# A two-layer graph network on one core: variances by five vector operations in place of 26, and twelve tiles of edge sums moved ahead of a wait

## The chip, the cores and the metric

The kernel runs on one core of a Trainium2 chip. The metric is the device time of one execution in microseconds; the time before is the median of three runs.

## The reference

```python
edge_index = stack([src, dst])                    # 3125 nodes, 53125 edges (loops among them), sorted by dst
h = maximum(layernorm(x), 0)                      # x is 3125 x 128; eps 1e-5
# layer 0: twelve steps of a network over the edges
h = tanh(h @ W_in + b_in)
deg = clip(segment_sum(1, dst), 1)
for step in range(12):
    agg = segment_sum(h[src], dst) / deg
    diff = tanh(gelu(agg @ W1 + b1) @ W2 + b2)
    h = h + (diff - relu(clearance) * h) * 0.5
x = x + h
# layer 1: two graph convolutions with further self loops and degree norms
h = maximum(layernorm(x), 0)
h = relu(gcn_conv(h, G1, gb1)); x = x + gcn_conv(h, G2, gb2)

def layernorm(x): m = mean(x); v = var(x); return (x - m) / sqrt(v + eps)
```

## The kernel before

Nodes are cut into 25 tiles of 128 (the last has 53), and the tiles into seven groups (four tiles each, then three, then two). The sum over edges is a product with an adjacency matrix of counts, `adj`, which the kernel builds in SBUF from the edge list. Node values enter that product as two f16 parts, `hi` and `lo`, so a tile of sources costs two matmuls of 128x512 for one group of destinations.

**The entry.** The edge list is searched for the start of each of 625 windows of five destination nodes. Meanwhile VectorE takes BN_STATS of every tile of `x` (`row_statistics`, L1346): six numbers a row, which are count, mean and count times variance of the even and of the odd elements. `variances` (L1349 to L1353) turns them into mean and variance, 25 times BN_AGGR and one add of eps. ScalarE takes the root (L1150), VectorE its reciprocal and the shift (`norm_factors`, L1415 to L1419), and ScalarE (L1156) and GpSimd (L662) then normalize the rows. The helper `link` makes VectorE wait for its own last result.

**The batches.** 52 batches of 12 windows build `adj`. For each, VectorE writes one-hot columns (`one_hots`, L1447), TensorE multiplies them into three PSUM banks (`window`, L795), and ScalarE moves the banks into `adj` (`evict`, L1174). Even batches use banks 0 to 2, odd ones banks 3 to 5. Between the batches TensorE does the first layer of the network and, when `adj` is far enough, parts of the first step's edge sums: `first_sums(g, part)` (L812) adds tiles `part` of sources into the bank of group g. A 625th window is done alone at the end (L849) and moved by a short eviction (L1197). When that has ended (`s_last[2]`), DMAs are started from SP (L545, the row of inverse degrees for all partitions) and from ScalarE's queue (the copy of a short tile within `adj`, `s_pair`).

**The first step.** On TensorE follow, in program order: a load of a flag from SBUF into a register (L851, `value_load`), the branch on it (L853) over a path that this graph does not take, the wait for `s_last[2]`, a small product that numbers blocks of edges of the last group (L1025, into bank 5, `s_boff`), and tiles 12 to 23 of the third group (`first_sums(2, ...)`, 24 matmuls). Then `s_owner` is waited for, which VectorE's `block_owners` (L1561 to L1574) gives from the numbering, and the sums of the fourth group begin.

The steps 1 to 10 are a loop, step 11 and the two convolutions follow.

Of the kernel before, what the change touches and what calls it, by code (L numbers as in the profile page):

```python
# [24 lines left out]
ALU = mybir.AluOpType  # L25
# [5 lines left out]
FULL = NODES // P  # L31
LAST = NODES - FULL * P
TILES = FULL + 1
# [3 lines left out]
FEAT = 128  # L37
# [3 lines left out]
EPS = 1e-5  # L41
# [25 lines left out]
BATCHES = WINDOWS // BATCH  # L67
# [6 lines left out]
EARLY_FROM = LO_AT[0] + 2  # L74
EARLY_TILES = 2
EARLY_LATE = EARLY_TILES * (BATCHES - ENTRY_BATCHES)
EARLY_PARTS = [(0, FULL - 1), (0, FULL), (0, EARLY_LATE - FULL)]
assert 0 < EARLY_LATE - FULL < FULL
assert EARLY_FROM + FULL <= ENTRY_BATCHES
PACK = 4096  # L80
# [8 lines left out]
OPEN = 1  # L89
# [15 lines left out]
SETS = PLACES // 2  # L105
SET_NODES = 2 * PLACE_NODES
# [5 lines left out]
def gnn_kernel(nc, x, src, dst, W_in, b_in, W1, b1, W2, b2, clearance, G1, gb1, G2, gb2, out):  # L112
    ctx = ExitStack()
    with ctx:
# [62 lines left out]
        ln_a = col(TILES)  # L177
        ln_b = col(TILES)
# [7 lines left out]
        def early_col(n, like=guess_and_stats):  # L186
# [4 lines left out]
        tail_first, tail_bound, tail_found, tail_start, tail_blocks, tail_mask2 = (  # L191
            early_col(SETS)[0:SET_NODES, :] for _ in range(6))
# [27 lines left out]
        stats = scratch[:, o:o + TILES * 6].rearrange("p (k s) -> p k s", s=6)  # L220
# [6 lines left out]
        tail_order = act_out[0:SET_NODES, o:o + SET_NODES]  # L227
# [148 lines left out]
        s_ev = [sem(f"windows_stored{u}") for u in range(2)]  # L376
# [354 lines left out]
        def _(pe):  # L731
# [60 lines left out]
            def window(buf, w, bank, place):  # L792
                b, i_ = w // RUN, w % RUN
                target = bank[:, 0:BANK_WIN * WROW].rearrange("p (k c) -> p k c", k=TILES)
                return nc.tensor.matmul(target[:, :, place * WIN:(place + 1) * WIN], Lb[buf][:, b, :, i_],  # L795
                                        Rb[buf][:, b, :, i_].rearrange("p (k d) -> p k d", d=WIN),
                                        start=True, stop=True)
# [8 lines left out]
            def first_sums(g, part):  # L806
                c0, n = SPANS[g]
                for at in range(*part):
                    k = K_FIRST[at][0]
                    for values in (hi, lo):  # L810
                        if values is hi or k != SHORT:
                            mm = nc.tensor.matmul(ps[:, FIRST_BANK[g], 0:n], values[:, k, :], adj[:, k, c0:c0 + n],  # L812
                                                  start=(at == 0 and values is hi),
                                                  stop=(k == SHORT or (g == 0 and at == FULL - 2 and values is lo)))
                return mm
# [31 lines left out]
            pe.wait_ge(s_last[0], 1)  # L847
            pe.wait_ge(s_ev[0], BATCHES // 2 + OPEN)
            window(0, 0, ps[:, 0, :], 0).then_inc(s_last[1], 1)  # L849

            missed = pe.value_load(flag[0:1, 0:1], min_val=0, max_val=1)  # L851

# [152 lines left out]
            def first_step():  # L1005
                def rest_and_short(g):
                    c0, n = SPANS[g]
                    bank = ps[:, REST_BANK[g], 0:n]

                    if g == 0:  # L1010
                        k = K_FIRST[FULL - 1][0]
                        nc.tensor.matmul(bank, hi[:, k, :], adj[:, k, c0:c0 + n], start=True, stop=False)
                        nc.tensor.matmul(bank, lo[:, k, :], adj[:, k, c0:c0 + n], start=False, stop=False)
                    with pe.If(missed != 0):
                        with pe.Fori(0, TILES) as r:
                            add_rest(0, g, bank, r)
                    nc.tensor.matmul(bank, hi[:, SHORT, :], adj[:, SHORT, c0:c0 + n], start=False, stop=True
                                     ).then_inc(s_agg, 1)

                def tail_check_sum():  # L1020
                    pe.wait_ge(s_valid, 1)
                    nc.tensor.matmul(ps[:, 2, 0:1 + CAP], ones_col.broadcast_to((P, P)), tail_check,
                                     start=True, stop=True).then_inc(s_checked, 1)

                nc.tensor.matmul(ps[0:SET_NODES, 5, 0:SETS], tail_order, tail_blocks, start=True, stop=True  # L1025
                                 ).then_inc(s_boff, 1)
                first_sums(2, (EARLY_PARTS[2][1], FULL))
                pe.wait_ge(s_owner, 1)
                for j in range(SETS):
                    nc.tensor.matmul(ps[:, 5, 16 + 4 * j:20 + 4 * j], owner[j], block_rows[:, j, :], start=True, stop=True)  # L1030
                    mm = nc.tensor.transpose(ps[:, 5, 64 + j * SET_NODES:64 + (j + 1) * SET_NODES], owner[j],
                                             ident[0:SET_NODES, 0:SET_NODES])
                mm.then_inc(s_ownerT, 1)
                first_sums(3, (0, 2 * HEAD))
                pe.wait_ge(s_pair, 16)
                for g in range(3):
                    rest_and_short(g)
                first_sums(3, (2 * HEAD, FULL))
                hidden(0, 0)
                rest_and_short(3)  # L1040
                first_sums(4, (0, HEAD))
                outputs(0, 0)
                hidden(0, 1)
                tail_check_sum()
                first_sums(4, (HEAD, 2 * HEAD))
                outputs(0, 1)
                hidden(0, 2)
                first_sums(4, (2 * HEAD, FULL))
                rest_and_short(4)
                outputs(0, 2)  # L1050
                hidden(0, 3)
                first_sums(5, (0, SPLIT))
                outputs(0, 3)
                hidden(0, 4)
                first_sums(5, (SPLIT, FULL))
                rest_and_short(5)
                first_sums(TAIL, (0, FULL))
                rest_and_short(TAIL)
                outputs(0, 4)
                hidden(0, 5)  # L1060
                hidden(0, TAIL)
                edge_sums(1, 0, (s_hi, s_lo), NG, (0, HEAD))
                outputs(0, TAIL - 1)
                outputs(0, TAIL)
                pe.wait_ge(s_tflag, 1)
# [221 lines left out]
        def _(dve):  # L1287
            chain = [0]

            def link(ins):  # L1290
                chain[0] += 1
                ins.then_inc(s_v, 1)
                dve.wait_ge(s_v, chain[0])
# [53 lines left out]
                return last_  # L1347

            def variances():  # L1349
                for k in range(TILES):  # L1350
                    last_ = V.bn_aggr(mv[:, k, :], stats[:, k, :])  # L1351
                link(last_)
                return V.tensor_scalar(ln_b[:, :], mv[:, :, 1], EPS, None, ALU.add)  # L1353

            def key_group(g):
                dve.wait_ge(s_wedges[g], 16)
# [58 lines left out]
            def norm_factors():  # L1415
                dve.wait_ge(s_std, 1)
                link(V.reciprocal(ln_a[:, :], ln_a[:, :]))
                V.scalar_tensor_tensor(out=ln_b[:, :], in0=mv[:, :, 0], scalar=-1.0, in1=ln_a[:, :], op0=ALU.mult,
                                       op1=ALU.mult).then_inc(s_ln, 1)  # L1419


# [465 lines left out]
```

## Time and profile before

| | |
|---|---|
| median of 3 runs | 1267.23 us (1266.03 to 1267.9) |
| the profiled execution | 1266.38 us, its span 1264.8 us |
| TensorE busy | 1227.2 us, 97% of the span |
| VectorE busy | 411.5 us |
| ScalarE busy | 306.4 us |
| GpSimd busy | 570.8 us |
| chain that ended last | TensorE 91%, VectorE 6% |

The profile has rows of what each engine did and when, in microseconds from the start of the span. The chain is followed back from the last instruction, at each step to what released it. PEclk is the granted clock of TensorE as a share of 2.4 GHz.

### The profile page before, as it was taken

How to read it: one execution, taken by the hardware profiler on the slowest of the kernel's cores; microseconds unless marked ns; L12 is line 12 of the kernel's file. 1: busy time of each engine (PE TensorE's matmuls, PEld its weight loads, DVE VectorE, ACT ScalarE, POOL GpSimd, SP SyncE). 2: the span in 40 equal slices, each digit the busy share in tenths (PEclk: the TensorE clock that was granted, in tenths of full speed). 3: DMA queues.
4: the chain of work that ended last, by engine and by line, in shares of the span. 5: the costliest groups of instructions: out<-in, count | busy, mean ns of one | idle time of the engine just before them, and what ended most of it. 6: DMA issues, size and time to landing. Idle time of an engine off the chain costs nothing.

```text
span 1264.8 us, 17221 instructions
## 1 busy us (share of the span) xinstructions
PE 1227.2 (97%) x6757; PEld 695.0 (55%) x6757; DVE 411.5 (33%) x853; ACT 306.4 (24%) x455; POOL 570.8 (45%) x426
## 2 busy tenths in 40 slices
PE   3899999999999999999999999999999999999998
PEld 1776565564564655645556456455564564555645
DVE  7999323131130231311302214113122142382412
ACT  1898222130131221301312113113131131130100
POOL 6700104827718448277284481772845818600000
PEclk8799999999999999999999999999999999999999
DMA  4000211222222312222222222231222223420101
GB/s 103 3 1 1 66 34 37 36 56 40 35 59 35 56 38 35 58 36 34 60 35 54 40 35 59 35 47 47 36 52 42 35 58 67 92 62 1 52 17 35
DMA packets 106136, 54.58 MB, mean 43 GB/s; under 512 B 13238, under 2 KB 104473, under 8 KB 105964
## 3 DMA queue, kind: packets, MB, share of 16 engines
q0 software_dynamic: 46352, 23.46, 14.4%
q1 hardware_dynamic: 57958, 29.48, 8.7%
q10 hardware_dynamic: 1782, 1.06, 0.3%
q8 instruction: 26, 0.43, 0.1%
q14 instruction: 18, 0.15, 0.0%
HBM read 32.53 MB, written 21.04 MB: 42 GB/s over the span
## 4 chain that ended last, share of the span: by engine, by line
PE 91%; DVE 6%; issue 1%; DMA 1%; ACT 1%; POOL 0%; DVEq 0%; ACTq 0%; POOLq 0%
PE ps L907 63%; PE ps L971 11%; PE ps L961 10%; PE ps L812 4%; DVE scratch L1447 3%; PE ps L795 2%; PE ps L1082 1%; PE ps L950 1%; DMA adj<-packed_scratch,adj 1%; DVE adj L1301 0%; DVE state L1730 0%; DVE lo L1430 0%; DVE cols L1351 0%; DVE adj L1392 0%; ACT adj L1174 0%
## 5 line engine op out<-in xcount | busy, mean ns | idle before, releaser
L907 PE MATMUL ps<-adj,hi 128*128 128x512 f16 (+2 forms) x2000 | 710.7, 367 | 0.0
L907 PE MATMUL ps<-adj,lo 128*128 128x512 f16 (+2 forms) x1920 | 693.8, 367 | 0.0
L684 POOL DMA_INDIRECT scratch<-state_scratch,tail_rows x264 | 390.6, 1480 | 390.4 <-DMA state_scratch<-state 313.2
L907 PEld LDWEIGHTS ps<-adj,hi 128*128 128x128 f16 x2000 | 194.3, 97 | 218.1 <-issue 12.9
L907 PEld LDWEIGHTS ps<-adj,lo 128*128 128x128 f16 x1920 | 186.8, 97 | 213.2 <-issue 14.6
L1622 DVE TENSOR_TENSOR ps<-ps,bias 128x512 f32<-128x512 f32 (+2 forms) x84 | 53.8, 641 | 488.9 <-PE ps L971 488.9
L1219 ACT ACTIVATE scratch<-ps 128x512 f32<-128x512 f32 (+2 forms) x84 | 46.3, 552 | 574.3 <-DVE ps L1622 573.3
L1210 ACT ACTIVATE scratch<-ps,b1c,cols 128x512 f32<-128x512 f32 (+2 forms) x156 | 107.3, 740 | 176.9 <-PE ps L961 176.1
L971 PEld LDWEIGHTS ps<-w,scratch 128*128 128x128 f32 (+1 forms) x1152 | 138.4, 190 | 14.0 <-issue 5.3
L971 PE MATMUL ps<-w,scratch 128*128 128x128 f32 (+1 forms) x1152 | 143.6, 276 | 0.1
L684 POOL DMA_INDIRECT entry<-state_scratch,tail_rows x88 | 129.7, 1474 | 26.8 <-issue 26.8
L961 PE MATMUL ps<-scratch,w 128*128 128x512 f32 (+2 forms) x336 | 137.8, 538 | 0.0
L1615 DVE TENSOR_TENSOR scratch<-ps,scratch 128x512 f32<-128x512 f32 (+1 forms) x72 | 47.6, 661 | 180.9 <-PE ps L961 130.5
L1447 DVE TENSOR_TENSOR scratch<-scratch 128x1536 f16<-128x1536 f16 (+1 forms) x106 | 91.7, 938 | 0.3 <-PE ps L795 0.3
L961 PEld LDWEIGHTS ps<-scratch,w 128*128 128x128 f32 x336 | 58.9, 190 | 37.8 <-issue 28.7
L1174 ACT ACTIVATE adj<-ps 128x1500 f16<-128x1500 f32 (+1 forms) x52 | 76.0, 1478 | 9.6 <-PE ps L795 9.3
L1629 DVE SCALAR_TENSOR_TENSOR state<-state,cols,scratch 128x512 f32<-128x512 f32 (+2 forms) x84 | 58.3, 694 | 49.7 <-ACT scratch L1219 49.5
L795 PE MATMUL ps<-scratch 128*128 128x125 f16 x625 | 56.9, 253 | 9.2 <-DVE scratch L1447 8.1
L1430 DVE SCALAR_TENSOR_TENSOR lo<-state,cols,hi 128x512 f16<-128x512 f32 (+2 forms) x91 | 59.9, 672 | 9.5 <-ACT hi L1110 8.8
L795 PEld LDWEIGHTS ps<-scratch 128*128 128x128 f16 x625 | 47.6, 112 | 24.4 <-DVE scratch L1447 21.3
L1110 ACT ACTIVATE hi<-state,cols 128x512 f16<-128x512 f32 (+2 forms) x84 | 53.2, 671 | 19.5 <-PE ps L950 11.7
L812 PE MATMUL ps<-adj,hi 128*128 128x512 f16 (+2 forms) x167 | 57.1, 354 | 0.0
(218 smaller groups left out, 420.3 us busy)
## 6 DMA issues: line engine op xcount, KB each, us to landing
state_scratch<-state SPq DMA_DIRECT2D x55, 256.0 KB, 2.3
scratch<-state_scratch,tail_rows POOLq DMA_INDIRECT x264
state_scratch<-state SPq DMA_DIRECT2D x11, 192.0 KB, 2.0
scratch<-rdeg_scratch SPq DMA_DIRECT2D x1, 1562.5 KB, 8.8
entry<-state_scratch,tail_rows POOLq DMA_INDIRECT x88
state<-in_x_dram SPq DMA_DIRECT2D x5, 256.0 KB
scratch<-in_x_dram SPq DMA_DIRECT2D x5, 256.0 KB
x_scratch<-state SPq DMA_DIRECT2D x5, 256.0 KB, 3.7
```

What stands on the lines that cost most here:

```text
L684: nc.gpsimd.indirect_dma_start(tail_sum[i], None, state_dram, bass.IndirectOffsetOnAxis(ap=tail_rows[:, at:at + 1], axis=0), compute_op=AL ...
L795: return nc.tensor.matmul(target[:, :, place * WIN:(place + 1) * WIN], Lb[buf][:, b, :, i_], Rb[buf][:, b, :, i_].rearrange("p (k d) -> p ...
L812: mm = nc.tensor.matmul(ps[:, FIRST_BANK[g], 0:n], values[:, k, :], adj[:, k, c0:c0 + n], start=(at == 0 and values is hi), stop=(k == SHO ...
L907: return nc.tensor.matmul(bank, values[:, k, :], adj[:, k, c0:c0 + n], start=is_first, stop=is_last)
L961: nc.tensor.matmul(ps_hid_tail[h] if g == TAIL else ps_hid[h][:, 0:n], w1[:, h * FEAT:(h + 1) * FEAT], agg[g == TAIL][:, 0:n], start=True, ...
L971: mm = nc.tensor.matmul(ps_out[g == TAIL][0:m, i * FEAT:(i + 1) * FEAT], hid_of(g, h)[:, i * P:i * P + m], w2[:, h, :], start=(h == 0), st ...
L1174: nc.scalar.activation(adj[:, :, bass.ds((i * 2 + u) * BATCH * WIN, BATCH * WIN)].rearrange("p k (b c) -> p b k c", b=BANKS), ps[:, 3 * u: ...
L1210: nc.scalar.activation(hid_of(g, h)[:, 0:n], ps_hid_tail[h] if g == TAIL else ps_hid[h][:, 0:n], ACT.Gelu, bias=b1c[:, h:h + 1], scale=now ...
L1430: return V.scalar_tensor_tensor(out=lo[:, k0:k1, :], in0=values[:, k0:k1, :], scalar=0.0 if factor is None else factor, in1=hi[:, k0:k1, : ...
L1447: last_ = V.tensor_tensor(buf[:, 0:b, :, 0:w], c_.broadcast_to((128, b, m, w)), k_.broadcast_to((128, b, m, w)), ALU.is_equal)
L1622: V.tensor_tensor(p_, p_, bias_of(1, nt), ALU.add).then_inc(s_bias, 1)
L1629: V.scalar_tensor_tensor(out=tiles_of(state, g), in0=tiles_of(state, g), scalar=now_keep, in1=act_out[:, 0:n_], op0=ALU.mult, op1=ALU.add) ...
```

## The change

Two edits. `variances` computes mean and variance of all 25 tiles at once from the six numbers: sum and difference of the two half means, sum of the two second moments, the difference squared times 32, and their sum divided by 128. What it leaves as the mean is twice the mean, and `norm_factors` multiplies by -0.5 in place of -1. The block numbering and tiles 12 to 23 of the third group stand ahead of the load of the flag and of the wait for the last eviction; they wait for the last odd eviction (`s_ev[1]`), which frees bank 5.

```diff
-EARLY_PARTS = [(0, FULL - 1), (0, FULL), (0, EARLY_LATE - FULL)]
+EARLY_PARTS = [(0, FULL - 1), (0, FULL), (0, FULL)]
...
             window(0, 0, ps[:, 0, :], 0).then_inc(s_last[1], 1)
+            pe.wait_ge(s_ev[1], BATCHES // 2 + OPEN)
+            nc.tensor.matmul(ps[0:SET_NODES, 5, 0:SETS], tail_order, tail_blocks, start=True, stop=True
+                             ).then_inc(s_boff, 1)
+            first_sums(2, (EARLY_LATE - FULL, FULL))
 
             missed = pe.value_load(flag[0:1, 0:1], min_val=0, max_val=1)
...
-                nc.tensor.matmul(ps[0:SET_NODES, 5, 0:SETS], tail_order, tail_blocks, start=True, stop=True
-                                 ).then_inc(s_boff, 1)
-                first_sums(2, (EARLY_PARTS[2][1], FULL))
                 pe.wait_ge(s_owner, 1)
...
             def variances():
-                for k in range(TILES):
-                    last_ = V.bn_aggr(mv[:, k, :], stats[:, k, :])
-                link(last_)
-                return V.tensor_scalar(ln_b[:, :], mv[:, :, 1], EPS, None, ALU.add)
+                mean_e, mean_o, dev_e, dev_o = (stats[:, :, i] for i in (1, 4, 2, 5))
+                V.tensor_tensor(mv[:, :, 0], mean_e, mean_o, ALU.add)
+                V.tensor_tensor(ln_b[:, :], dev_e, dev_o, ALU.add)
+                link(V.tensor_tensor(ln_a[:, :], mean_e, mean_o, ALU.subtract))
+                link(V.scalar_tensor_tensor(out=ln_a[:, :], in0=ln_a[:, :], scalar=FEAT / 4, in1=ln_a[:, :], op0=ALU.mult,
+                                            op1=ALU.mult))
+                link(V.tensor_tensor(ln_b[:, :], ln_b[:, :], ln_a[:, :], ALU.add))
+                return V.tensor_scalar(ln_b[:, :], ln_b[:, :], 1 / FEAT, EPS, ALU.mult, ALU.add)
...
-                V.scalar_tensor_tensor(out=ln_b[:, :], in0=mv[:, :, 0], scalar=-1.0, in1=ln_a[:, :], op0=ALU.mult,
+                V.scalar_tensor_tensor(out=ln_b[:, :], in0=mv[:, :, 0], scalar=-0.5, in1=ln_a[:, :], op0=ALU.mult,
                                        op1=ALU.mult).then_inc(s_ln, 1)
```

On VectorE, between the end of the statistics and the second batch of one-hots (`cols` holds `mv`, `ln_a` and `ln_b`, `scratch` the statistics and the one-hots), this stood before:

```order
L1346 BN_STATS scratch<-state 128x6 x2
L1363 TENSOR_SCALAR adj<-adj 128x125 [waits slot_edges_ready]
L1364 TENSOR_SCALAR adj<-adj 128x125
L1351 BN_AGGR cols<-scratch 128x2 [waits vector_chain]
L1351 BN_AGGR cols<-scratch 128x2 x24
L1353 TENSOR_SCALAR cols<-cols 128x25 [waits vector_chain]
L1447 TENSOR_TENSOR scratch<-scratch 128x1536 [waits windows_multiplied0,window_keys_copied,one_hot_counts_made]
L1447 TENSOR_TENSOR scratch<-scratch 128x1500
L1417 RECIPROCAL cols<-cols 128x25 [waits deviations_ready]
```

and this stands there now:

```order
L1347 BN_STATS scratch<-state 128x6 x2
L1368 TENSOR_SCALAR adj<-adj 128x125 [waits slot_edges_ready]
L1369 TENSOR_SCALAR adj<-adj 128x125
L1352 TENSOR_TENSOR cols<-scratch 128x25 [waits vector_chain]
L1353 TENSOR_TENSOR cols<-scratch 128x25
L1354 TENSOR_TENSOR cols<-scratch 128x25
L1355 SCALAR_TENSOR_TENSOR cols<-cols 128x25 [waits vector_chain]
L1357 TENSOR_TENSOR cols<-cols 128x25 [waits vector_chain]
L1358 TENSOR_SCALAR cols<-cols 128x25 [waits vector_chain]
L1452 TENSOR_TENSOR scratch<-scratch 128x1536 [waits windows_multiplied0,window_keys_copied,one_hot_counts_made]
L1452 TENSOR_TENSOR scratch<-scratch 128x1500
L1422 RECIPROCAL cols<-cols 128x25 [waits deviations_ready]
```

26 instructions with one wait between them have become six with three waits between them; nothing around them has moved.

On TensorE, from the last window (bank 0) to the block owners, this stood before (the first gap is the path that is branched over, the second the other 22 matmuls of tiles 12 to 23):

```order
L795 MATMUL ps<-scratch 128x25x5 [waits windows_stored0,last_window_one_hots]
L851 TENSOR_LOAD flag
L851 ISA x2
L853 COMPARE_AND_BRANCH
...
L1025 MATMUL ps<-cols,scratch 92x2 [waits weights_loaded,last_window_stored]
L812 MATMUL ps<-adj,hi 128x512
L812 MATMUL ps<-adj,lo 128x512
...
L1030 MATMUL ps<-cols,scratch 128x4 [waits tail_block_owners_ready]
```

and this stands there now (the first gap is the other 22 matmuls, the second the path that is branched over):

```order
L795 MATMUL ps<-scratch 128x25x5 [waits windows_stored0,last_window_one_hots]
L851 MATMUL ps<-cols,scratch 92x2 [waits windows_stored1]
L812 MATMUL ps<-adj,hi 128x512
L812 MATMUL ps<-adj,lo 128x512
...
L855 TENSOR_LOAD flag
L855 ISA x2
L857 COMPARE_AND_BRANCH
...
L1031 MATMUL ps<-cols,scratch 128x4 [waits tail_block_owners_ready,weights_loaded,last_window_stored]
```

The numbering product and 24 matmuls have moved from behind the load, the branch and the wait for the last window's eviction to ahead of all three, behind a wait for the last odd batch's eviction.

## Rows read from the trace of the kernel before

**Rows 1.** The page: busy time of the engines and share of the span.

```profile
PE 1227.2 (97%) x6757; PEld 695.0 (55%) x6757; DVE 411.5 (33%) x853; ACT 306.4 (24%) x455; POOL 570.8 (45%) x426
```

**Rows 2.** Busy time by stretch: length, busy time of each engine, PEclk, DMA share, GB/s.

```profile
53.00:100.00 47.00, 42.43 (x411) 33.17 (x411) 46.95 (x57) 45.05 (x44) 5.48 (x3) 0.98 0.04 2
100.00:134.00 34.00, 32.15 (x301) 21.80 (x301) 31.51 (x39) 29.02 (x22) 0.00 (x0) 1.00 0.00 1
300.00:1200.00 900.00, 899.87 (x4654) 493.58 (x4653) 232.25 (x493) 175.69 (x295) 464.30 (x313) 1.00 0.26 46
```

**Rows 3.** The chain that ended last, 28 to 56 us: start, length, what.

```profile
29.43 1.67 DVE cols L1351 x25
...
44.34 1.21 PE ps L795 x12
...
46.39 0.86 PE ps L795 x12
```

**Rows 4.** VectorE in order of time, 27 to 44.5 us: start, length, what.

```profile
29.34 1.75 DVE L1351 BATCH_NORM_AGGREGATE cols<-scratch 128x2 f32<-128x6 f32 x25
31.12 0.18 DVE L1353 TENSOR_SCALAR cols<-cols 128x25 f32<-128x25 f32 x1
31.23 1.81 DVE L1447 TENSOR_TENSOR scratch<-scratch 128x1536 f16<-128x1536 f16 x2
...
40.24 0.18 DVE L1398 COPY adj<-ps 125x25 f32<-125x25 f32 x1
40.46 0.18 DVE L1399 TENSOR_TENSOR adj<-ps,adj 125x25 f32<-125x25 f32 x1
...
41.53 0.18 DVE L1410 TENSOR_REDUCE cols<-adj 125x1 f32<-125x25 f32 x1
41.62 0.17 DVE L1411 TENSOR_SCALAR adj<-adj 125x25 f32<-125x25 f32 x1
```

**Rows 5.** ScalarE's root in order of time, with its idle time before and the releaser.

```profile
31.34 0.22 ACT L1150 ACTIVATE cols<-cols 128x25 f32<-128x25 f32 x1 [1.37 <-DVE cols L1353]
```

**Rows 6.** TensorE by stretch: length, busy time, PEclk, DMA share, GB/s.

```profile
44.00:45.00 1.00, 0.74 (x8) 0.60 0.00 0
...
51.00:52.00 1.00, 1.00 (x13) 0.82 0.00 0
...
55.00:56.00 1.00, 1.00 (x14) 0.98 0.00 0
```

**Rows 7.** All engines in order of time around the last evictions, 128 to 140 us.

```profile
132.32 1.48 ACT L1174 ACTIVATE adj<-ps 128x1500 f32 x1 [0.23 <-PE ps L795]
...
132.87 0.23 PE L795 MATMUL ps<-scratch 128*128 128x125 f16 x1
133.69 0.31 ACT L1197 ACTIVATE adj<-ps 128x125 f16<-128x125 f32 x1
...
134.05 0.32 PE L1025 MATMUL ps<-cols,scratch 92*92 92x2 f32 x2 [0.95 <-ACT adj L1197]
...
136.44 0.22 DVE L1571 TENSOR_SCALAR cols<-cols 92x2 f32<-92x2 f32 x1
```

**Rows 8.** TensorE's sequencer: duration in ns (min/median/max), first and last start.

```profile
L851 PEldq TENSOR_LOAD <-flag x1: 496/496/496, 132.3 to 132.3; - x1
...
L853 PEldq COMPARE_BRANCH  x1: 367/367/367, 133.1 to 133.1; - x1
...
L1014 PEldq COMPARE_BRANCH  x7: 200/207/323, 143.4 to 188.5; - x7
```

**Rows 9.** What the first step needs next: times of use, and a DMA's landing.

```profile
142.88 0.15 DVE L1642 TENSOR_SCALAR cols<-cols 128x1 f32<-128x1 f32 x1 [6.22 <-DMA scratch<-rdeg_scratch]
...
147.32 0.81 PE L1017 MATMUL ps<-adj,hi 128*128 128x512 f16 x3
...
adj<-adj ACTq DMA_DIRECT2D x1, 390.6 KB, 9.1
```

**Rows 10.** The chain again, 128 to 148 us: the 24 matmuls.

```profile
134.38 5.21 PE ps L812 x24
```

## The prediction

> **What bounds the kernel now.** I read the page first: TensorE is busy for 1227.2 us, 97% of the span [rows 1]. The stretches say where it is not the whole story: from 300 to 1200 us TensorE is busy for 899.87 of 900 us, so nothing in the loop of steps can take up or give back a shift that comes from ahead of it [rows 2]. From 53 to 100 us it is VectorE that has no room, 46.95 of 47 us, and from 100 to 134 us TensorE with 32.15 of 34 [rows 2]. The reader is to see a relay: VectorE sets the pace until about 100 us, TensorE from there to the end. Both edits lie ahead of the loop, one in VectorE's part, one at the end of the construction of the adjacency matrix. So a microsecond gained on the relay comes out at the end, and a microsecond gained beside it is worth nothing. The third view, the chain, tells which of the two holds: the 25 BN_AGGR stand on it, 1.67 us from 29.43 on [rows 3]. The fourth is the order of time around the last evictions, where TensorE stands idle for 0.95 us until the last window has been moved, and then starts the block numbering at 134.05 [rows 7].
>
> **First edit, the variances: -0.94 us.** Before, the first BN_AGGR starts at 29.34, the add of eps at 31.12, and the one-hots at 31.23 [rows 4]: from the first BN_AGGR to the one-hots 1.89 us. (BN_AGGR costs 1.78 / 26 = 0.068 us each in a row, the wait counted as one more.) After, six instructions on 128x25 f32 stand there. Nearest rows: two operations on 125x25 f32 with a wait for the first's result start 0.22 us apart (40.24, 40.46), two without such a wait 0.09 us apart (41.53, 41.62) [rows 4]. The new order is mean, moments, difference (two steps of 0.09), then three waited steps of 0.22 to the square, the sum and the last scaling, then 0.11 to the one-hots as at 31.12 before: 2 x 0.09 + 3 x 0.22 + 0.11 = 0.95 us. Saved: 1.89 - 0.95 = 0.94 us. No row has these operations reading every sixth element of the statistics. The bounds: BN_AGGR reads six elements in 0.068 us, so that a stride of 24 bytes would have to cost much to show in 25 elements; if each of the three reading ops took 0.1 more, 0.3 would be gone, and if the waited steps took 0.20 in place of 0.22, 0.06 would be added. I take 0.94, bounds 0.6 and 1.0.
>
> The factor -0.5 for -1 in the shift costs nothing: it is the same instruction with another constant.
>
> Does all of it arrive? What stands behind the variances on VectorE moves up by 0.94 with it. The one-hots' other inputs were there long before. ScalarE waited 1.37 us for the variances, more than the 0.94 that it is now given them earlier [rows 5], so its root does not become the limit, nor the reciprocal behind the first one-hots. The rows' normalization on ScalarE and GpSimd waits for VectorE's factors and moves up too. From 44 to 53 us the chain runs over TensorE and ScalarE for a while (12 windows at 44.34 and at 46.39 [rows 3]), but these were all released by VectorE's earlier work, so that stretch moves as a whole. From 53 us on VectorE is full. I see nothing on the way that is tied to the start of the program, except the clock (a rival, below).
>
> **Second edit, the order on TensorE: -0.20 us.** Before, TensorE's matmuls ended at 133.10 (0.23 from 132.87) and resumed at 134.05, 0.05 after the last window's eviction ended (133.69 + 0.31 = 134.00) [rows 7]. After, the numbering waits for the last odd batch's eviction instead, the one that starts at 132.32 and takes 1.48 us [rows 7]: 133.80, and with the same 0.05 the numbering starts at 133.85. That is 0.20 earlier, and the 24 matmuls that follow, the fourth group and the whole first step come earlier by as much. The bounds: 0.10, if the handover takes 0.15, and 0.30, if the bank is given free when the next eviction starts at 133.69. The 0.95 us hole does not close, since the eviction of the last odd batch ends only 0.20 us before that of the last window: both are on ScalarE, one behind the other.
>
> What is moved past: the load of the flag, its two register operations and the branch, which stood in the hole. They ran on the sequencer from 132.3 to 133.1 and the branch 0.37 more [rows 8], together 1.17 us, with nothing lost, since the wait lasted until 134.0. Now they come behind 24 matmuls. Would TensorE run dry during them? The sequencer runs ahead of the array: the first branch at L1014 is done at 143.4, and the matmul behind it in the program starts at 147.32 [rows 8, 9], a lead of 3.9 us. That branch itself stood behind a wait for a copy that was started as the last window's eviction ended and took 9.1 us to land (134.0 + 9.1 = 143.1 [rows 7, 9]), so the lead could have been larger. At the new place the lead starts from nothing at 133.85, because the sequencer waits there. It then has 24 matmuls to gain it, which last 5.21 us on the array, 0.217 each [rows 10]. How fast it issues is bounded by the same branch: four small and 34 large matmuls after the owners were ready at 136.66 (136.44 + 0.22 [rows 7]) and before 143.4 [rows 8] are 6.7 / 38 = 0.18 us each at most. At that slowest rate the lead is 24 x 0.037 = 0.9 us, and 0.3 of the 1.17 would show; at half the time a matmul the lead is 3.0 us and nothing shows. I take nothing, since the 6.7 us contain a wait of unknown length, and keep 0.3 for the range and 1.17 for a rival.
>
> What waits behind: VectorE's block owners wait for the numbering and for the last window's eviction, so they can start at 134.0 and end before 136.66, while TensorE needs them only 5.5 us after the numbering's start. The DMAs that start with the last window's eviction do not move: the inverse degrees arrive at 142.88 and are used after TensorE's 147.32, the copy lands at 143.1 and is needed there too [rows 9]. Both have four microseconds, and TensorE comes 0.2 sooner. No stall takes the place of the one shortened.
>
> **The sum.** -0.94 - 0.20 = -1.14 us. Against the profiled execution's own 1266.38 us that is 1265.2. That run was 0.85 us below the median of 1267.23, so for the median I forecast 1267.23 - 1.14 = 1266.1 us. This is 0.09%; a measurement of this kernel can tell about 0.2%, 2.5 us, from no change.
>
> **The rivals.** *The clock does not move with the work (12 in 100).* TensorE is granted 1.2 GHz until about 44.8 us and 2.4 GHz after that (the mean of 44 to 45 us is 0.60, which is 0.8 at half and 0.2 at full), and a second low stretch goes from 51.6 (0.82 over 51 to 52) to just past 55 (0.98 over 55 to 56) [rows 6]. If the rise stays at 44.8 while the work comes 0.94 earlier, that much more of it runs at half speed: 0.47 us is given back, as the 12 windows at 44.34, half in the low clock, took 1.21 where those at 46.39 took 0.86 [rows 3]. The net is -0.67, 1266.6 us. Against it: the second low stretch would then take the work at 51 us less. The Trainium skill, TensorE: Matmul & The Clock Gate, Part 1, has the monitor's window "free-running", not started by the kernel; by it the rise need not follow the work, and one trace alone does not show whether it does.
>
> *The second low stretch shrinks or is gone (8 in 100).* Moved against the work, the fall at 51.6 may hit less of it or not come. A batch of windows there would gain 0.35 us to twice that (1.21 against 0.86): 1265.4 to 1265.7.
>
> *The flag's load is not hidden (8 in 100).* If the sequencer must see the matmuls out before it loads the register, 1.17 us show, the sum is +0.03 and the time 1267.3. For it: in the trace of before the load stands in a hole, and its row can't tell whether it would have made one. Against it: the lead of 3.9 us at a branch.
>
> *Slower: the clock's rise is missed once (4 in 100).* If the shift makes the rise come later by as much as the second low stretch lasts (3.4 us), the windows, entry products and transposes from 44.3 to 47.3 take twice their time, +2.7 us, and the net is +1.5: 1268.8 us. It turns the sign as soon as 1.14 us are lost; for slower by over 0.2% it would take 3.7 us. Against it: TensorE's work ahead of the rise keeps its form and only moves.
>
> **How the numbers follow.** The forecast has 68 in 100, its own range 1265.0 to 1267.2 us (bounds of the terms, 0.3 for the load, and a run spread of 0.8 to each side). The range takes in the clock and the load as rivals and the spread beyond them: 1264.2 to 1268.0. Faster by over 0.2% (below 1264.7) needs a bias of over a microsecond beside the sum: 7 from the forecast's spread and 2 from the rival with gains, 0.09. Slower by over 0.2% (above 1269.8) has 0.03. The rest is 0.88.
>
> **What would show it.** In the profile after: six small operations on VectorE over 0.8 to 0.95 us and the one-hots at about 30.3; the clock's rise at about 43.9 if it follows the work, at 44.8 if not; TensorE's handover from VectorE near 99.3 in place of 100.2; the numbering at 132.9 (133.85 less 0.94), a hole of 0.75 us ahead of it; the load of the flag with no idle time of TensorE behind tile 23; the matmul of L1017 at 146.2; a loop as long as before. Wrong would be: a hole behind the 24 matmuls, a VectorE that waits between 29 and 53 us for ScalarE or GpSimd, or steps whose length changed.

## The result: 0.47% slower

The kernel after takes 1273.03 us (median of 6 runs, 1272.61 to 1274.14), the kernel before 1267.57 us in the same comparison (6 runs, 1265.87 to 1269.3). The ratio is 1.0047, 95% interval 1.0037 to 1.0057: 5.5 us slower by the medians, where 1.1 us faster was forecast. A hole behind the 24 matmuls was what the prediction had named as the sign of being wrong, and it is there. The profiled execution took 1274.14 us, its span 1272.5 us.

The page of the kernel after answers to [rows 1]. TensorE is busy for the same 1227.2 us; the span has grown around it:

```profile
span 1272.5 us, 17201 instructions
PE 1227.2 (96%) x6757; PEld 693.9 (55%) x6757; DVE 411.2 (32%) x833; ACT 306.2 (24%) x455; POOL 566.3 (45%) x426
```

The stretches of the kernel after (from and to, length, busy time and count of PE, PEld, DVE, ACT and POOL, PEclk, DMA share, GB/s) say where. The loop is as full as in [rows 2], and from 134 to 150 us TensorE works for only 10.38 of 16 us:

```profile
134.00:150.00 16.00, 10.38 (x46) 4.59 (x44) 2.79 (x15) 1.23 (x2) 2.41 (x3) 0.89 0.44 127
...
300.00:1200.00 900.00, 899.91 (x4655) 493.58 (x4653) 229.02 (x486) 174.58 (x293) 470.73 (x318) 1.00 0.26 45
```

The chain of the kernel after (start, length, what) puts the hole behind the 24 moved matmuls. The last odd eviction ends, the numbering starts at once, the matmuls run 5.21 us as in [rows 10], and then 4.88 us pass before the block owners' product:

```profile
133.55 1.49 ACT adj L1175
135.03 0.04 issue
135.08 0.32 PE ps L851 x2
135.40 5.21 PE ps L812 x24
140.61 4.88 issue
145.49 0.36 PE ps L1031 x2
...
155.30 0.65 PE ps L1021 x3
```

"Issue" means that the profile shows nothing that was waited for. VectorE's owners were long there (its last operation on them started at 137.46 and took 0.22 us). The rows of TensorE's sequencer (PEldq; it takes TensorE's instructions in program order) in the kernel after, which answer to [rows 8], name the holder: the branch on the flag, 0.37 us before, took 7.88 us from 137.4 on. It ended at 145.3, and the next matmul started at 145.49:

```profile
L855 PEldq TENSOR_LOAD <-flag x1: 487/487/487, 136.6 to 136.6; - x1
...
L857 PEldq COMPARE_BRANCH  x1: 7882/7882/7882, 137.4 to 137.4; - x1
```

The DMA engines during that branch, in two windows of the kernel after (queue, kind: packets, MB, share of 16 engines). From 137.4 to 142 us q1, SP's broadcast, and q10, the copy of the short tile, have 99.7% of them:

```profile
q1 hardware_dynamic: 103, 1.29, 88.2%
q10 hardware_dynamic: 32, 0.20, 11.5%
```

Only from 142 to 145.3 us is there one packet of the kind that the view calls "instruction", here called a packet of code:

```profile
q10 hardware_dynamic: 48, 0.20, 21.7%
q1 hardware_dynamic: 18, 0.03, 2.8%
q8 instruction: 1, 0.02, 2.4%
```

A window from 142.6 to 142.8 us still has it. It moved 5.2 us after the branch began and 2.6 us before it ended:

```profile
q8 instruction: 1, 0.02, 40.2%
```

The first edit did what it should. It leaves six operations on 128x25: the title's five, and the last one, which scales and adds eps where an add of eps stood before. VectorE in the kernel after, as in [rows 4]; from the first operation at 30.28 to the one-hots at 31.27 are 0.99 us, where 1.89 were:

```profile
30.28 0.19 DVE L1352 TENSOR_TENSOR cols<-scratch 128x25 f32<-128x25 f32 x1
...
30.95 0.18 DVE L1357 TENSOR_TENSOR cols<-cols 128x25 f32<-128x25 f32 x1
31.17 0.57 DVE L1358 TENSOR_SCALAR cols<-cols 128x25 f32<-128x25 f32 x1
31.27 1.81 DVE L1452 TENSOR_TENSOR scratch<-scratch 128x1536 f16<-128x1536 f16 x2
```

The two profiled executions differ by 7.7 us of span. Piece by piece, after less before:

| stretch | before | after | difference |
|---|---|---|---|
| start to the variances' first operation (nothing changed there) | 29.34 | 30.28 | +0.94 |
| variances to the first one-hots | 1.89 | 0.99 | -0.90 |
| first one-hots to the last odd eviction's start (the clock, below) | 101.09 | 102.28 | +1.19 |
| last odd eviction's start to the numbering | 1.73 | 1.53 | -0.20 |
| numbering to the block owners' product | 5.54 | 10.41 | +4.87 |
| block owners' product to the first rest sums on the chain | 7.90 | 9.81 | +1.91 |
| sum | | | +7.81 |

The +1.91 is the hole's second price. Behind it TensorE runs at half clock for a while (from and to, length, busy time of PE, PEclk, DMA share, GB/s):

```profile
146.00:148.50 2.50, 2.50 (x9) 0.50 0.03 7
```

The first and the third line belong to the execution and not to the change: over the traces below, the third is 100.75 to 104.49 us in seven kernels with the new variances and 100.78 to 104.33 in four with the old, and the first is 28.74 to 30.28 and 28.43 to 29.58. The other four make -0.90 - 0.20 + 4.87 + 1.91 = +5.7 us, against +5.5 between the medians.

### The profile page after: what moved, and what is told of

It is laid out like the page before. It is cut to its first block, busy times and chain, and to the rows that moved or that the text cites. A ratio compares the mean times of both kernels' runs of the same rounds, so it can differ in the third digit from the quotient of the medians.

```text
span 1272.5 us, 17201 instructions
## 1 busy us (share of the span) xinstructions
PE 1227.2 (96%) x6757; PEld 693.9 (55%) x6757; DVE 411.2 (32%) x833; ACT 306.2 (24%) x455; POOL 566.3 (45%) x426
## 4 chain that ended last, share of the span: by engine, by line
PE 91%; DVE 6%; issue 2%; DMA 1%; ACT 1%; POOL 0%; DVEq 0%; ACTq 0%; POOLq 0%
PE ps L911 62%; PE ps L975 11%; PE ps L965 10%; PE ps L812 4%; DVE scratch L1452 3%; PE ps L795 2%; PE ps L1083 1%; PE ps L954 1%; DMA adj<-packed_scratch,adj 1%; DVE adj L1302 0%; ACT adj L1175 0%; DVE state L1735 0%; DVE lo L1435 0%; DVE adj L1397 0%; ACT scratch L1211 0%
## 5 line engine op out<-in xcount | busy, mean ns | idle before, releaser
L975 PEld LDWEIGHTS ps<-w,scratch 128*128 128x128 f32 (+1 forms) x1152 | 138.4, 190 | 13.9 <-issue 5.3
```

Source lines behind the costliest of these rows:

```text
L975: mm = nc.tensor.matmul(ps_out[g == TAIL][0:m, i * FEAT:(i + 1) * FEAT], hid_of(g, h)[:, i * P:i * P + m], w2[:, h, :], start=(h == 0), st ...
```

## The experiments

Time is compared with runs of the kernel before on the same chip. The table has what the single parts below rest on; "branch" is the duration of the branch on the flag on TensorE, "target" the row of the listing of TensorE's program at which it lands. Each kernel has one trace, of one of its runs, and the columns between the name and the ratio come from it.

| kernel | branch at | target | branch, us | hole behind the matmuls | ratio (95% interval) |
|---|---|---|---|---|---|
| before | 133.1 | 438 | 0.37 | none | 1 |
| after | 137.4 | 487 | 7.88 | 4.88 | 1.0047 (1.0037, 1.0057) |
| variances alone | 132.6 | 438 | 0.37 | none | 0.9985 (0.9976, 0.9995) |
| order alone | 138.1 | 487 | 7.47 | 4.84 | 1.0051 (1.0037, 1.0065) |
| branch first | 131.3 | 438 | 0.37 | none | 0.9993 (0.9983, 1.0003) |
| tiles fill the hole | 132.3 | 438 | 0.37 | none | 0.9990 (0.9981, 0.9999) |
| broadcast held | 139.5 | 487 | 3.85 | 1.85 | 1.0003 (0.9993, 1.0013) |
| short general path | 135.8 | 296 | 0.22 | none | 0.9991 (0.9981, 1.0000) |
| general path as before | 138.4 | 463 | 0.37 | 1.18, later | 1.0001 (0.9991, 1.0011) |
| long path, old order | 135.5 | 462 | 0.37 | none | 0.9997 (0.9987, 1.0007) |
| longer path, old order | 133.1 | 488 | 3.79 | 3.07, ahead | 1.0040 (1.0029, 1.0051) |
| both DMAs held | 136.4 | 487 | 3.37 | 0.37 | 1.0017 (1.0006, 1.0028) |

**Each edit by itself.** The first kernel is the one after with this undone:

```diff
-EARLY_PARTS = [(0, FULL - 1), (0, FULL), (0, FULL)]
+EARLY_PARTS = [(0, FULL - 1), (0, FULL), (0, EARLY_LATE - FULL)]
...
-            pe.wait_ge(s_ev[1], BATCHES // 2 + OPEN)
-            nc.tensor.matmul(ps[0:SET_NODES, 5, 0:SETS], tail_order, tail_blocks, start=True, stop=True
-                             ).then_inc(s_boff, 1)
-            first_sums(2, (EARLY_LATE - FULL, FULL))
...
+                nc.tensor.matmul(ps[0:SET_NODES, 5, 0:SETS], tail_order, tail_blocks, start=True, stop=True
+                                 ).then_inc(s_boff, 1)
+                first_sums(2, (EARLY_PARTS[2][1], FULL))
                 pe.wait_ge(s_owner, 1)
```

> Only the five operations for the variances; TensorE's order as before. Theory: the kernel after lost its time at the branch on the flag, which took 7.88 us (0.37 before), and the variances gained about 0.9 us. So here about 0.9 us below the kernel before, from the statistics' end to the first one-hots 0.99 us (1.89 before), and a branch of about 0.4 us. Rival: the earlier work meets the clock of TensorE worse (the chain from 31 to 100 us took 1.2 us longer after than before), and the kernel is 0.3 us or more above the kernel before.

It took 1265.83 us (11 runs) against 1267.53 (27 runs): 0.15% faster, 0.6 to 3.0 us by the interval. The sum's 0.94 lies within, and its profiled execution shows the branch at 0.37 us. The variances gain; they are not the loss.

The second kernel has BN_AGGR and the factor -1 back and keeps TensorE's new order:

```diff
-                mean_e, mean_o, dev_e, dev_o = (stats[:, :, i] for i in (1, 4, 2, 5))
...
+                for k in range(TILES):
+                    last_ = V.bn_aggr(mv[:, k, :], stats[:, k, :])
+                link(last_)
+                return V.tensor_scalar(ln_b[:, :], mv[:, :, 1], EPS, None, ALU.add)
```

> Only the order on TensorE (numbering and 24 matmuls ahead of the load and the branch); variances by BN_AGGR as before. Theory: all of the loss is here, -0.2 us for the earlier numbering, +4.9 for the hole at the branch, +1.8 for a stretch of half clock behind it: +6.4 us on the kernel before, with a branch of 7 to 8 us. Rival, the loss is made elsewhere (variances, clock): within 1 us of the kernel before, and a branch of less than 5 us.

It took 1274.82 us (5 runs) against 1267.53 (27 runs). The ratio makes this +0.51%, or 6.5 us, and its chain has the same hole:

```profile
135.69 5.21 PE ps L812 x24
140.90 4.84 issue
145.74 0.56 PE ps L1031 x2
```

The whole loss is in the order.

**The branch at its old time.** The moved work stays ahead of the wait for the last window's eviction, but the load and the branch stand ahead of the work again:

```diff
-EARLY_PARTS = [(0, FULL - 1), (0, FULL), (0, FULL)]
+EARLY_PARTS = [(0, FULL - 1), (0, FULL), (0, EARLY_LATE - FULL)]
...
             window(0, 0, ps[:, 0, :], 0).then_inc(s_last[1], 1)
-            pe.wait_ge(s_ev[1], BATCHES // 2 + OPEN)
-            nc.tensor.matmul(ps[0:SET_NODES, 5, 0:SETS], tail_order, tail_blocks, start=True, stop=True
-                             ).then_inc(s_boff, 1)
-            first_sums(2, (EARLY_LATE - FULL, FULL))
 
             missed = pe.value_load(flag[0:1, 0:1], min_val=0, max_val=1)
...
                 pe.wait_ge(g_apair, 16)
+
+            pe.wait_ge(s_ev[1], BATCHES // 2 + OPEN)
+            nc.tensor.matmul(ps[0:SET_NODES, 5, 0:SETS], tail_order, tail_blocks, start=True, stop=True
+                             ).then_inc(s_boff, 1)
+            first_sums(2, (EARLY_LATE - FULL, FULL))
```

> Both edits, but with the load of the flag and the branch ahead of the moved numbering and matmuls, so the branch comes at the time of before, when no large DMA is on the way; the wait for the last window's eviction stays behind the matmuls. Theory: branch of about 0.4 us, no hole behind the 24 matmuls, 1.1 us below the kernel before. Rival: it is the numbering's place ahead of the eviction or the longer queue of matmuls that costs, not the branch's time; then a hole of several us at the block owners, and 5 us above the kernel before.

The edit puts the target back to row 438 as well. Time and target go back together here, so this kernel does not tell which of the two counts. Its chain is what the forecast drew, numbering 1.53 us after the last odd eviction's start and no hole:

```profile
130.48 1.49 ACT adj L1176
131.97 0.04 issue
132.01 0.32 PE ps L893 x2
132.33 5.21 PE ps L812 x24
137.55 0.12 PE ps L1032 x2
```

From the eviction's start to the owners' product it takes 7.07 us, where the variances alone, with the old order, take 7.27 (131.83 to 139.10): the 0.20 of the sum. In time it is 1266.25 us (11 runs), 0.07% faster, an interval that holds both the 1.1 us and no change.

**The wait filled.** Four of the twelve tiles go ahead of the wait for the bank (against the kernel with the branch first):

```diff
+            first_sums(2, (EARLY_LATE - FULL, EARLY_LATE - FULL + 4))
             pe.wait_ge(s_ev[1], BATCHES // 2 + OPEN)
             nc.tensor.matmul(ps[0:SET_NODES, 5, 0:SETS], tail_order, tail_blocks, start=True, stop=True
                              ).then_inc(s_boff, 1)
-            first_sums(2, (EARLY_LATE - FULL, FULL))
+            first_sums(2, (EARLY_LATE - FULL + 4, FULL))
```

> As the kernel with the branch first, and four of the twelve tiles stand ahead of the wait for the last odd eviction (they need no bank that it frees): 8 matmuls of 0.217 us fill the 0.75 us that TensorE would wait. Theory: hole ahead of the numbering gone but for the sequencer's load and branch (it ends at about 133.5, 0.4 us after the last window's matmul), so another 0.4 us gained: 1.5 us below the kernel before. Rival: the code behind the branch is not there yet at 133.5 and no more is gained than by the branch first: 1.1 us below.

The chain shows 0.47 us left, in which the load and the branch end:

```profile
132.22 0.07 PE ps L795
132.29 0.47 issue
132.76 1.91 PE ps L812 x8
134.67 0.09 PE ps L894 x2
134.75 3.48 PE ps L812 x16
138.24 0.12 PE ps L1033 x2
```

From the last window's matmul to the owners' product are 6.18 us (132.06 to 138.24), and 6.51 with the branch first (131.04 to 137.55): 0.33 gained where 0.4 was expected. 1266.38 us (11 runs) and a ratio of 0.9990 are not to be told from the kernel with the branch first.

**Contention or the branch itself.** SP waits for the transposed owners ahead of the broadcast:

```diff
             sp.wait_ge(s_last[2], 1)
+            sp.wait_ge(s_ownerT, 1)
             sp.dma_start(row, rdeg_dram.rearrange("(a n) -> a n", a=1).broadcast_to((128, NODES))
```

> The kernel after, but SP starts the broadcast of the inverse degrees (1.6 MB, about 9.8 us) only when TensorE has transposed the block owners, so it is not on the way while the branch is taken; the copy of the short tile (0.4 MB) still is. Theory A, the branch waits for its target's code, and that fetch stands behind the broadcast in the DMA engines: branch of at most 3 us, its end before the 24 matmuls are done, hole under 0.5 us, and within 2 us of the kernel before (the broadcast lands some 5 us later and VectorE may wait for it). Theory B, the branch costs what it costs behind a filled queue of matmuls whatever the DMAs do: 7 to 8 us again, hole of 4.9 us, 6 us above the kernel before.

Each theory missed some of its numbers. The branch fell from 7.9 to 3.85 us, so theory B is out; but 3.85 is more than A's 3. The hole was still 1.85 us, as a load of the flag of 1.50 us came ahead of the branch (0.49 to 0.83 in the other kernels). In time A was right: 1268.59 us and 1.0003 are no change. The trace is of its slowest run, 1272.14 us, so the hole may be shorter in the others.

The copy of the short tile was to be still on the way, and it was not. It had the DMA engines during the load, and by the branch it was through (139.5 to 143.4 us):

```profile
q8 instruction: 1, 0.02, 1.5%
q10 hardware_dynamic: 2, 0.00, 0.0%
```

**Both DMAs held,** the copy of the short tile too:

```diff
             act.wait_ge(s_last[2], 1)
+            act.wait_ge(s_ownerT, 1)
             act.dma_start(adj[STACK:P, SHORT, :], adj[0:STACK, SHORT, :]).then_inc(s_pair, 16)
```

> The kernel after, with the broadcast and the copy of the short tile both started only when the block owners are transposed, so that no DMA but the fetch itself is on the way at the branch. Theory, fetch and queueing apart: 7.9 us with both DMAs, 3.8 with the copy alone, and here 1.5 to 3 us, which ends before the 24 matmuls are done: no hole behind them. In time near the kernel before, as both DMAs land 5 us later and TensorE may wait for the copy. Rival, the fetch alone takes the 3.8 us and the copy had no part in it: branch of 3.5 to 4 us.

The branch took 3.37 us, above the theory's 3 and under the rival's 3.5. As the copy was over before the branch of the kernel above, both kernels show the branch with next to nothing else on the way, at 3.37 and 3.85 us, and no run here gives the copy a price. From 136.4 to 139.8 us the DMA engines moved a single packet:

```profile
q8 instruction: 1, 0.02, 1.8%
```

It moved at 137.4, 1.0 us after the branch began (1.5 with the broadcast held, 5.2 in the kernel after), and the branch ended 2.3 to 2.6 us behind it in all three. So what the two transfers added is nearly all time before the packet of code moved.

The load began at 135.5, 4.1 us before the last of the 24 matmuls ended, and load and branch together took 4.3: the cover is just too short. The time, 1269.65 us, has another cause that was foreseen: TensorE waited for the copy, which now landed at 150.39.

**Which code is missing.** First the path that this graph branches over is left out of TensorE's program:

```diff
             with pe.If(missed != 0):
-                pe.wait_ge(s_last[2], 1)
-                for g in (1, 2):
-                    if EARLY_PARTS[g][1]:
...
-                for g in (1, 2):
-                    first_sums(g, EARLY_PARTS[g])
                 pe.wait_ge(g_apair, 16)
```

> The kernel after, with the path that this graph branches over left out of TensorE's program (191 rows of the listing), so that the branch's target is the next instruction but one; all DMAs as after. Theory A (the fetch of far code waits): branch of 0.2 to 0.4 us, no hole, 1.1 us below the kernel before. Theory B (the branch waits for the matmuls ahead of it or for the DMAs themselves): 7 to 8 us and the hole again, 6 us above.

With the same executed work and the same DMAs the branch takes 0.22 us and there is no hole. The kernel takes 1266.24 us (10 runs), 1.3 us less than before by the medians, with an interval that ends at no change. A branch behind a filled queue, during a broadcast, is not slow as such; this one is slow because of where it goes.

Then the path gets back its old length, with the place of the branch as after (it leaves out tiles 12 to 23 of the third group, which a graph on this path would need):

```diff
-EARLY_PARTS = [(0, FULL - 1), (0, FULL), (0, FULL)]
+EARLY_PARTS = [(0, FULL - 1), (0, FULL), (0, EARLY_LATE - FULL)]
```

> The kernel after, with 24 matmuls fewer in the path that is branched over, so that its length is that of before (only that path, which this graph does not take, is incomplete). Theory: it is the time of the branch, within the broadcast, that costs: 7 to 8 us, hole of 4.9 us, 6 us above the kernel before. Rival: the path has outgrown what is fetched ahead, and with the old length the branch takes 0.4 us and the kernel is 1.1 us below the kernel before.

This overturned my theory that the time of the branch alone decides. It is taken at 138.4, inside the broadcast, and takes 0.37 us. The edit to `EARLY_PARTS`, which I had not costed since this graph never runs that path, had moved the target from row 463 to 487. More code seems to come late further on: the matmuls of the fourth group stop once for 1.18 us.

```profile
144.32 0.38 PE L812 MATMUL ps<-adj,hi 128*128 128x512 f16 x1
145.89 0.38 PE L812 MATMUL ps<-adj,lo 128*128 128x512 f16 x1 [1.18 <-issue]
```

A packet of code moved just before, from 143.2 to 143.4 us, 2.6 us ahead of the matmul at 145.89, which is the distance from packet to branch's end above; that this stop is a wait for code is read from that alone:

```profile
q8 instruction: 1, 0.02, 36.9%
```

1268.76 against 1267.57 us, a ratio of 1.0001, is no change, and neither the theory's 6 us slower nor the rival's 1.1 us faster.

The counterpart lengthens the path in the kernel before, by the 24 matmuls:

```diff
-EARLY_PARTS = [(0, FULL - 1), (0, FULL), (0, EARLY_LATE - FULL)]
+EARLY_PARTS = [(0, FULL - 1), (0, FULL), (0, FULL)]
...
-                first_sums(2, (EARLY_PARTS[2][1], FULL))
+                first_sums(2, (EARLY_LATE - FULL, FULL))
```

> The kernel before, with the path that is branched over as long as after (24 matmuls more in it, which this graph does not run). Theory, time and not length: branch of 0.4 us at about 133, as before, and no change in time. Rival, length: the target must be fetched, 1 to 2 us, and as it is started at 133 it may also meet the broadcast: a branch of over 1 us, TensorE later by that less the wait that covers it, 0.5 us or more above the kernel before.

The branch takes 0.37 us, and the time does not change. The path is as long as in the kernel after, so with the target at row 462 length alone does nothing. The last kernel therefore goes on to row 488, with 26 further matmuls in the path (a graph that took this path would have tiles added twice, here and in the kernel before this one):

```diff
                 for g in (1, 2):
                     first_sums(g, EARLY_PARTS[g])
+                first_sums(2, (0, 13))
```

> The kernel before, with 50 matmuls more in the path that is branched over (24 as in the run with the long path, 26 more), so that the branch's target stands where it stood in the kernel after, 488 rows into TensorE's listing, while the branch is where it was before. This graph does not run that path. Theory: what decides is whether the target's code had been fetched when the branch is taken, thus its place in the program. Then the branch takes 3 to 8 us here too, where it took 0.37 with the target at row 462, TensorE starts the numbering 2.5 us or more after the last window's eviction, and the kernel is 2 to 8 us above the kernel before, though nothing in its executed work has changed. Rival: it needs the later time (the broadcast under way, matmuls queued) as well: branch of 0.4 us and no change in time.

Nothing that this graph executes differs from the kernel before, and it is 0.40% slower: 1272.77 us (10 runs) against 1267.14 (19 runs). The branch takes 3.79 us at its old time:

```profile
L853 PEldq COMPARE_BRANCH  x1: 3792/3792/3792, 133.1 to 133.1; - x1
```

and the chain has its hole ahead of the numbering, and behind it 24 matmuls in 7.62 us in place of 5.21, with a mean PEclk of 0.79 over 134 to 150 us:

```profile
133.94 3.07 issue
137.02 0.44 PE ps L1026 x2
137.46 7.62 PE ps L812 x24
```

3.1 + 2.4 = 5.5 us, the 5.6 of the medians. The place of the target in the program makes a loss by itself. Here the packet of code moved at 134.05, 0.95 us after the branch began and ahead of the broadcast's first data; behind the broadcast, in the kernel after, the branch took twice as long.

## Why the prediction was wrong

- **The variances: right.** 0.95 us were forecast for the six operations and 0.99 measured, so -0.90 for -0.94; the steps without a wait took 0.11 each in place of 0.09. Alone they make the kernel 0.6 to 3.0 us faster, an interval that holds the 0.94.
- **The numbering earlier: right.** 0.20 forecast, 0.20 measured; the hole ahead of it is 0.74 us, 0.75 forecast. The loop did not change.
- **What is moved past: this step failed,** at "I take nothing" for the load and the branch, "keep 0.3 for the range and 1.17 for a rival". The half on the lead was right: the sequencer had issued the 24 matmuls at 136.6, 1.5 us after the numbering, and had 4.0 us in hand. The half on the price was wrong: I took the branch at the 0.37 us of its old place, and in the kernel after it took 7.88. So 4.9 us showed, and 1.9 of half clock behind them. Its duration depends on whether the target's code is there. The target had moved in the listing from row 438 to 487, by the 25 rows that I watched and by the 24 of `EARLY_PARTS[2]` that I had read as a bookkeeping of a path not taken. Either shift alone leaves the branch at 0.37 us (rows 462, 463), both together do not. The long branch takes 3.4 to 3.9 us with next to nothing else on the DMA engines, and 4 more with the broadcast of 1.6 MB and the copy under way. That it waits for code to be fetched rests on the one q8 packet inside each long branch, with 2.3 to 2.8 us from it to the branch's end, and on the four kernels that change only code which this graph does not run; the view does not name the engine that a packet of code is for. How many rows are held, and where a block ends, no run shows beyond this: rows up to 463 were there and row 487 was not.
- **The Trainium skill,** Runtime: NRT & Kernel Launch, section Instruction fetch mechanics, has this rule: a taken branch whose target lies outside the two blocks of code held must fetch the block first. The kernels with the target at rows 487 and 488 agree, with 3.4 to 7.9 us. I had weighed its page on the clock and not this one. What it calls mostly hidden, the running on into a next block, seems to have cost 1.18 us during the broadcast.
- **The rivals.** The one on the load and the branch had the right place and a price 5 us too small. The slower one, a low stretch of clock during start-up, has the right sign by chance: the half clock of 1.91 us stands behind the hole, a cause that it did not name. That the clock's rise need not follow the work held: the clock rose at 36.8 us, and neither at 43.9 nor at 44.8, and fell again at 40 for ten microseconds (below).
- **The range,** 1264.2 to 1268.0, had bounds for each duration at its old place, and none for a duration that changes with the place.

Both gains together, with the branch ahead of the moved work, give 1266.25 us, the variances alone 1265.83: the experiments do not tell these apart, nor the tiles in the hole. All are 1 to 2 us below the kernel before by their medians.

## What to carry to other kernels

When a branch over a long path moves, or the path or the code ahead of it grows, its duration in the old trace is no price: ask where its target lies in the program and what DMAs are under way. Load and branch together took 4.3 us with idle DMA engines and 8.7 behind the broadcast, and the queued work must last that long from the load's start. Take such a branch ahead of the transfers and not behind them, and count code that never runs, too, since it moves what does. A hole in TensorE can also cost some 2 us of half clock behind it. It did behind holes of 4.88, 4.84, 3.07 and 1.85 us. It did not with both DMAs held, where TensorE stood for 2.8 us until 150.4 and PEclk stayed at 1.00, so its length alone does not tell:

```profile
150.40:152.00 1.60, 1.56 (x8) 1.00 0.00 0
```

## What I had not expected of the hardware

- **Unexecuted code changed the time by 0.40%.** A branch of 0.37 us (target at row 438 or 462) became one of 3.79 us (row 488), in the same executed program.
- **The clock's low stretches move from execution to execution.** In the kernel after, the rise at 36.8 us lasted until 40.2 only, and PEclk was 0.51 from 40 to 50 us. With the broadcast held, the same work up to here, PEclk was 0.50 until 44, rose, and was 0.50 again from 52 to 58 us. In [rows 6] the low stretches end at 44.8 and 55 us.

```profile
37.00:40.00 3.00, 3.00 (x46) 1.00 0.01 3
40.00:50.00 10.00, 7.46 (x50) 0.51 0.04 3
50.00:51.00 1.00, 1.00 (x13) 0.78 0.54 12
```

  In the profile of the long path with the old order, PEclk is 0.60 from 53 to 60 us, and its last odd eviction comes 2.3 us later than before (134.65 against 132.32). The kernel before itself goes from 1266.03 to 1270.38 us over 31 runs. That the low stretches make this spread is plausible from their size; no run here was made to show it.
- **The last small operation of the variances,** multiply and add on 128x25, took 0.57 us where its neighbours took 0.18, and ScalarE's root waited for it until 31.77. It is not on the chain. Its predecessor in [rows 4], an add alone, took 0.18. Why was not tried.
- **The load of a flag into a register** took 0.49 to 0.50 us in eight of the profiled executions. In four it took 0.71, 0.72, 0.83 and 1.50 us. In these four the DMA engines were full during the load (one queue alone has a share of 0.91 to 1.31; over such short windows the view can pass 1); in the kernel after, with 0.49, the share was 0.54, and in the others nothing large had begun. The 1.50 us fell together with the copy of the short tile, the shorter three with the broadcast. No run was made to test it.
